# Scatters of expert rows issued in pairs over each attention slot and over six shared blocks, in place of one burst each

## The reference

```python
x = x + cross_attention(layernorm(x), ctx_1024, ctx_1024, mask, heads=16)      # 8 x 512 x 1024 scores a head
# feed-forward on xf = layernorm(x), 4096 tokens:
ys = geglu(xf @ Ws1 + bs1) @ Ws2 + bs2                                         # the shared expert, hidden size 512
top_val, top_idx = top_k((xf @ Wr + br) / 1.5, 2);  top_w = softmax(top_val)   # 2 of 12 experts for each token
yE = geglu(xf @ We1[e] + be1[e]) @ We2[e] + be2[e]                             # an expert e, hidden size 768
x = x + ys + sum over the two chosen experts of top_w * yE
```

## Time and profile before

| what | before |
|---|---|
| runs | 1084.34 to 1089.44 us, median 1086.86 |
| profiled execution, span | 1085.2 us |
| PE busy | 957.5 us (88%) |
| DVE, ACT, POOL busy | 714.1, 569.3, 373.7 us |
| DMA | 117.34 MB, mean 108 GB/s |

### The profile page before, as it was taken

One profiled execution on the slowest core, in us unless ns is written; L12 is line 12 of the kernel. 1 busy time (PEld: TensorE's weight loads), 2 busy tenths in 40 slices (PEclk: granted clock), 3 DMA queues, 4 the chain that ended last, 5 costly groups with the idle time before them and its releaser, 6 DMA issues.

```text
span 1085.2 us, 26548 instructions
## 1 busy us (share of the span) xinstructions
PE 957.5 (88%) x7515; PEld 696.9 (64%) x7515; DVE 714.1 (66%) x1842; ACT 569.3 (52%) x1276; POOL 373.7 (34%) x537
## 2 busy tenths in 40 slices
PE   5588899989888887979399889999989999999996
PEld 4233445535354344758188778888768888898885
DVE  5776778878676735646078557776636677667753
ACT  3136565655545565323054457667535667657653
POOL 5300212344443453132700044445323345335342
PEclk9779999999999999989589989999999999999999
DMA  4552315263362142144463473545324355435332
GB/s 152 132 105 81 95 55 137 90 149 86 104 157 62 41 144 74 60 148 150 153 221 117 140 216 52 140 123 144 48 33 128 49 139 138 94 85 138 48 54 42
DMA packets 107927, 117.34 MB, mean 108 GB/s; under 512 B 20396, under 2 KB 99960, under 8 KB 107648
## 3 DMA queue, kind: packets, MB, share of 16 engines
q1 hardware_dynamic: 87168, 67.97, 23.4%
q0 software_dynamic: 20064, 47.20, 17.6%
q10 hardware_dynamic: 560, 0.53, 0.1%
HBM read 73.91 MB, written 38.87 MB: 104 GB/s over the span
## 4 chain that ended last, share of the span: by engine, by line
PE 40%; issue 5%; DMA 3%; DVE 3%; another core or an unknown queue 2%; ACT 1%; DVEq 1%; SPq 0%; ACTq 0%; POOL 0%; POOLq 0%
PE ff_psH L2300 24%; PE ff_psY L2327 13%; PE ff_psX L2254 2%; DVE ff_actf L2553 1%; PE ff_psH L2269 1%; DMA out_dram<-ff_x 1%; DMA ff_xrow<-expert_in 1%; DMA expert_in<-ff_zeros 1%; PE ff_psY L2284 1%; DVE ff_actl L2546 1%; DMA ff_x<-out_dram 1%; ACT ff_gel L2394 0%; DVE ff_ysb L2629 0%; DVE ff_x L2570 0%
## 5 line engine op out<-in xcount | busy, mean ns | idle before, releaser
L2300 PE MATMUL ff_psH<-xh,ff_wx 128*128 128x256 f16 (+1 forms) x1776 | 271.0, 264 | 15.1 <-issue 9.7
L1126 DVE TENSOR_REDUCE fast_negm<-fast_psS 128x2 f32<-128x512 f32 x256 | 168.5, 686 | 85.0 <-PE fast_psS L514 75.4
L2300 PE MATMUL ff_psH<-xl,ff_wx 128*128 128x256 f16 (+1 forms) x888 | 218.7, 264 | 0.0
L886 ACT ACTIVATE fast_PT<-fast_psT 128x512 f32<-128x512 f32 x256 | 147.3, 596 | 119.9 <-PE fast_psT L546 102.2
L2235 POOL DMA_INDIRECT out_dram<-ff_ysc,ff_trow x78 | 125.6, 1610 | 194.0 <-ACT ff_ysc L2442 175.4
L2300 PEld LDWEIGHTS ff_psH<-xh,ff_wx 128*128 128x128 f16 x1776 | 167.5, 99 | 37.2 <-issue 13.9
L2553 DVE SCALAR_TENSOR_TENSOR ff_actf<-ff_psH,ff_b1T,ff_gel 128x256 f32<-128x256 f32 (+1 forms) x234 | 106.0, 454 | 101.4 <-ACT ff_gel L2394 99.7
L2394 ACT ACTIVATE ff_gel<-ff_psH,ff_b1T 128x256 f32<-128x256 f32 (+1 forms) x234 | 105.4, 451 | 82.5 <-PE ff_psH L2300 62.8
L514 PE MATMUL fast_psS<-fast_Kz,fast_Qs 128*128 128x512 f16 x256 | 101.8, 403 | 35.1 <-DVE fast_negm L1126 25.0
L2327 PE MATMUL ff_psY<-ff_wx,ff_acth 128*128 128x256 f16 x792 | 132.2, 273 | 0.6 <-DVE ff_actl L2546 0.5
L2389 ACT ACTIVATE ff_acth<-ff_actf 128x256 f16<-128x256 f32 (+1 forms) x282 | 110.5, 392 | 33.3 <-DVE ff_actf L2553 31.3
(11 more groups left out here) (276 smaller groups left out, 1672.6 us busy)
## 6 DMA issues: line engine op xcount, KB each, us to landing
ff_st<-in_L_ffn_We_dram POOLq DMA_DIRECT2D x12, 1536.0 KB
ff_xrow<-expert_in SPq DMA_DIRECT2D x41, 256.0 KB
ff_st<-in_L_ffn_We_dram POOLq DMA_DIRECT2D x12, 768.0 KB
fast_Qs<-qstk SPq DMA_DIRECT2D x48, 128.0 KB
fast_xbuf<-in_x_dram SPq DMA_DIRECT2D x8, 512.0 KB, 5.1
fast_words<-in_mask_BxSxS_bk_dram SPq DMA_DIRECT2D x8, 512.0 KB, 3.7
fast_xres<-in_x_dram SPq DMA_DIRECT2D x8, 512.0 KB, 4.1
out_dram<-fast_x1s SPq DMA_DIRECT2D x8, 512.0 KB, 5.1
```

Source lines behind the costliest of these rows:

```text
L886: nc.scalar.activation(PT[:, n % NPT, :], psT[n % 2][:], ACT.Exp).then_inc(sem["exp_done"], 1)
L1126: nc.vector.tensor_reduce(negm[:, two(b), t, 2 * p:2 * p + 2], src, AX.X, ALU.max, negate=True).then_inc(sem["max_done"], 1)
L2300: mm = nc.tensor.matmul(psH[j % stage.banks][:, (half + 1) * NB - rows:(half + 1) * NB], a[:, dt, lo:lo + P], x[:, dt, NB - rows:], start= ...
```

## The change

In each slot of POOL, `rows_out` and `meta` move to the front, behind `rstd2_`, and the eight scatters go out in four pairs: behind `meta`, behind `keep_x1`, and two behind `res_bias` that wait for the 11th and the 17th exponential of batch b. In `feed_forward()` each of the 12 pairs waits for a gate of its own: two pairs a block in blocks 2 to 7 (`act` in place of `y_mm`). The value that `place_value` reads is masked to 17 bits, which doesn't change it.

```diff
@@ -1477,10 +1477,10 @@
                 ins = nc.gpsimd.tensor_tensor(x1s[:, t, :], xres[:, t, :], keep["bs2"][:], ALU.add)
             ins.then_inc(sem["acc_done"], 1)
 
-        def scatter(b):
+        def scatter(b, these=range(2 * QT)):
             until(pool, "place_link", of("place_link", b, 5), alone=True)
-            for t in range(QT):
-                for k in range(2):
+            for n in these:
+                    t, k = n // 2, n % 2
                     pool.indirect_dma_start(out=scratch["xs"][:, :],
                                             out_offset=bass.IndirectOffsetOnAxis(ap=pos[two(b)][:, k, t:t + 1], axis=0),
                                             in_=xn2_of(b)[:, t, :], in_offset=None, bounds_check=X_ROWS - 1)\
@@ -1564,21 +1564,32 @@
             return
 
         def slot(b):
+            moved = real(b - 3) and not left_over(b - 3)
+
+            def rows_of_two(j, after=None):
+                if moved:
+                    if after:
+                        until(pool, "exp_done", of("exp_done", b, after))
+                    scatter(b - 3, (2 * j, 2 * j + 1))
+
             if real(b - 2):
                 rstd2_(b - 2)
+            if real(b - 4) and not left_over(b - 4):
+                rows_out(b - 4)
+            if moved:
+                meta(b - 3)
+            rows_of_two(0)
             if real(b):
                 sum_words(b)
             if real(b + 3):
                 rstd1(b + 3)
             if real(b - 2):
                 keep_x1(b - 2)
+            rows_of_two(1)
             if real(b - 1):
                 res_bias(b - 1)
-            if real(b - 4) and not left_over(b - 4):
-                rows_out(b - 4)
-            if real(b - 3) and not left_over(b - 3):
-                meta(b - 3)
-                scatter(b - 3)
+            rows_of_two(2, 11)
+            rows_of_two(3, 17)
 
         constants()
         rstd1(0)
@@ -1824,7 +1835,7 @@
 PIECES = 2 * EX_PAIRS
 PIECE = WCOLS // PIECES
 NSH = N // NB - EARLY
-LEFT_FROM = 3
+LEFT_FROM = 2
 FIRST_PIECES = 4
 LAST_PIECES = FIRST_PIECES + PIECES // SH_PAIRS
 
@@ -1971,8 +1982,9 @@
         return rowmeta[:, bass.ds((n & 1) * NBT, NBT), :]
 
     def place_value(eng, e):
-        return nc.values_load(place_i[0:1, bass.ds(e, 1)], engines=[eng.engine], min_val=0, max_val=(NBLK * PLACE + PLACE) * OVER - 1,
+        value = nc.values_load(place_i[0:1, bass.ds(e, 1)], engines=[eng.engine], min_val=0, max_val=(NBLK * PLACE + PLACE) * OVER - 1,
                                skip_runtime_bounds_check_because="built on chip from counts whose sum is two rows a token")
+        return value & (PLACE * PLACE * OVER - 1)
 
     def place_of(eng, e, value=None):
         value = place_value(eng, e) if value is None else value
@@ -2197,8 +2209,8 @@
         nc.gpsimd.tensor_copy(last[:, :, D + 1], mix[2][:])
         nc.gpsimd.tensor_tensor(last[:, :, D + 2], mix[1][:], mix[2][:], ALU.subtract).then_inc(meta_link, 1)
         pool.wait_ge(meta_link, 6)
-        shared.until(pool, "y_mm", of(shared, "y_mm", LEFT_FROM))
         for t in range(LEFT * QT):
+            shared.until(pool, "act", of(shared, "act", LEFT_FROM + t // 2, t % 2 * (SH_PAIRS // 2)))
             for k in range(2):
                 pool.indirect_dma_start(out=xs[:, :], in_=keep["xn2"][:, NT - LEFT * QT + t, :], in_offset=None,
                                         out_offset=bass.IndirectOffsetOnAxis(ap=last_pos[:, k, t:t + 1], axis=0),
```

## The result

In the set of runs that the prediction is held against, the changed kernel took 1055.74 us, median of 4 runs (1054.67 to 1057.44), and the kernel before 1085.96, median of 4 (1084.34 to 1089.44). The ratio is 0.972, with a 95% interval of 0.9691 to 0.9748: 2.8% faster. The forecast was 1048 with a range of 1037 to 1073. Later sets on other chips, further down, show that this gain exists on some chips only; that is the main thing that the experiments found.

A forecast was written before the change was run, and what follows sets the result against it. Back-to-back scatter bursts were taken as the bound, making other engines late. From the profiled 1085.2 us, minus 26.4 (hole) and 17.7 (slots), plus 4.8 (pairs) and 0.6 (mask), gave 1046.5; plus 1.7 for the runs, 1048 us, range 1037 to 1073.

The forecast's parts named there:

- The present bound: Attention slots and shared stage: while many scatters are queued back to back, other engines get instructions or semaphores late.
- The hole: Shared stage: the block beside the burst of 24 scatters takes 35.10 us instead of 8.7; spreading them gains 26.4 us.
- The slots: Attention slots 3 to 7: 17.7 us gained without bursts, 12.7 in slots 3 to 5 and 5 in slots 6 and 7.
- Twelve pairs in the shared stage: Shared blocks: each of 12 scatter pairs costs 0.15 us in its new place, part of 4.8 us for all 32 pairs.
- scatters in twos: Sign that the forecast holds: after the change the scatters go out two at a time.
- The moved load of expert 1's weights: Shared stage: the load moves to the middle of block 7, about 543 us, 47 us before its use; cost 0.
- POOL's order in the slots: Attention slots: `meta` and pairs ahead of POOL's other work are covered by its existing waits; cost 0.
- the mask: Place value: one more register instruction per expert on PE, ACT and DVE, 0.05 us times 12, 0.6 us lost.
- Pairs keep a short burst's share: Rival, slots and shared stage: each of 32 pairs loses 0.97 us, 31 us in all, giving 1074 us; chance 0.14.
- The hole belongs to the place: Rival, shared stage: fetching code at PE's and DVE's loop entry causes the hole, so only slots gain; 1072 us, chance 0.06.
- Nothing changes: Rival: the loss goes with each scatter and is paid again wherever scatters stand; 1087 us, chance 0.07.
- Slower: Rival, 5 slots and 6 blocks: every pair stops the engines, 2.0 us each, 63 lost against 44.1 gained; 1106 us, chance 0.05.

The follow-up runs named there:

- e5: The kernel before with the mask on the place value as its only edit, on chip 13; 1048.96 us against 1048.95 for the kernel before, ratio 1.0009.
- e1: Changed kernel, but the shared stage scatters its 24 in one burst as before (pairs in the slots only), on chip 5; 1050.49 us, ratio 1.0018 to the kernel before.
- e6: The changed kernel, unchanged, run once more on chip 13; 1049.02 us, ratio 1.0004 to the kernel before.
- e4: Changed kernel with the load of expert 1's weights issued ahead of the shared stage's first pair, on chip 5; 1049.85 us, ratio 1.002 to the kernel before.
- e8: Changed kernel with the shared stage's 24 scatters in groups of four, eight and twelve, on chip 4; 1062.48 us beside 1084.04 for the kernel before, ratio 0.9789.

## Why the prediction was right, and where it was not

*The present bound.* Right for the profile that it was read from: the bursts stopped the other engines, and what they waited for was no data. I left open whether instructions or semaphores came late. For DVE's 21.5 us it was not the data, which had moved 19 us earlier; between its signal and its instructions the traces still can't choose. For PE a signal is not enough: twelve matmuls without a wait between them took 12.6 us in place of 1.2. It was wrong to take the stall for a property of the kernel. It belongs to the kernel on certain chips, and no view of one profile could have shown that.

*The hole, -26.4.* Measured -26.6.

*The slots, -17.7, less 20 pairs at 0.15, net -14.7.* Measured -15.1, with slot 3 to 5 at 44.4, 45.0 and 42.5 and the clock at 1.00. The sum hides two misses that cancel: slots 3 to 5 gained 12.5 us where 12.7 less 12 pairs, 10.9, was forecast, and slots 6 and 7 gained 2.6 where 5 less 8 pairs, 3.8, was. Slots 6 and 7 differ by more than that between kernels on calm chips (76.5 us in e5, 83.1 in e1), so that this agreement is partly luck.

*Twelve pairs in the shared stage, +1.8.* Too small. The windows from 3 to 9 take 54.9 us in the changed kernel's stalling profile and 51.7 in e6, the same program on chip 13: 3.2 us. The step that failed is "scatters in twos": from block 3 on they went in fours. That true pairs would have cost less there is argued, since no run had them.

*The moved load of expert 1's weights, 0.* This term failed, and it makes most of the miss: 7.0 us in one window, 5.4 with the next one, which is 1.6 shorter. I had asked only whether the weights come in time (they do; ACT converts them from 584 on) and not what 2.3 MB in flight do to others. SP's store of 256 KB took 10.5 us to land beside them. On chip 13 the same kernel has 13.03 and 10.10 us in these two windows where e4, with its load far ahead, has 8.87 and 11.87: 2.4 net. And e5, with the load one block earlier, loses 2.5 (11.34 against 8.87). So 2.5 us are the load's on a calm chip, with or without the change, and the stalling set has 5.4. In the kernel before no shared block after the hole shows any of it (8.35 to 8.88 us): it lay under the hole, a cover that the change took away.

*POOL's order in the slots, 0, and the mask, +0.6.* Slots of slot 2's length bear out the first; e5's ratio of 1.0009 (0.9982 to 1.0036) can't tell 0.6 us from nothing.

*The sum.* 1048 against 1055.7; of the profiled spans, 1046.5 against 1054.4, 7.9 us. The load makes 5.4 of them, the shared pairs 1.4 (3.2 for 1.8), the experts 1.8 (2.4 for 0.6), and the hole and the slots give back 0.6; the rest is rounding. For the experts' 2.4 no cause is shown; the stretch behind window 10 to 11, which they fill, takes 471.6 to 476.0 us in the other kernels, whose work there is the same.

*The rivals.* "Pairs keep a short burst's share" (1074) is out by the slots. "The hole belongs to the place" (1072) is out as it stood, by the 8.47 us window and by e8's 8.30; but a place acts together with the number in a way that I can't name. "Nothing changes" (1087) was right in its ratio on two sets that could test it, 1.0004 on chip 13 and, by halves, 1.0018 and 1.0003 on chip 5, and for a reason that the prediction didn't have: there is nothing to remove. "Slower" had a chance of 0.05; the changed kernel is slower in neither of its two sets (0.972, and 1.0004 with 0.9981 to 1.0028).

*What was to show it.* Right: slot lengths and clock, DVE's 21.5 us wait gone, and PE without an issue wait from 490 to 545 us. Wrong: "no shared block over 11 us" (15.88), and the wait for an unnamed releaser is gone only as the one long wait, with 8.5 us left in four; "scatters in twos" and "expert stage as long as before" (2.4 us longer) failed too.

## What to carry to other kernels

An idle time that ends on nothing the profile can name is a reason to look at a second chip before explaining it: here the same program took 1047 or 1084 us, and a change worth 2.8% on one was worth 0.0% on the other. When a step that hides a stall is taken away, list the transfers that ran under it, and ask of each whom it will hold up in the open: a load of 2.3 MB was early enough for its reader and still cost 5.4 us, and sent in six parts it cost next to nothing. A wait without a name is not yet a stall: see whether the same wait has a name in a run whose landings are on record. Spacing is worth what its gates make of it: look at how far apart they really lie against how long POOL needs for what stands behind each.

## What the runs showed of the hardware that was not expected

- On some chips, or in some sets, engines go on late while GpSimd's scatters are queued: DVE 19 us after the data of its load had moved, ACT 7.4 us behind PE, and PE itself with 12.6 us for twelve matmuls that wait for nothing between them. On the calm chips 5 and 13 the same 24 scatters in a row in the same place, at the same 1.28 us pitch, left PE busy for all of its 8.30 and 8.29 us.
- Where it happens it is not proportional to the scatters: 24 cost 26.6 us, eight 9, four 0.5, twelve at another place 0.9, and three pairs that stood alone 0.2 together.
- In the stalling sets landings are missing from the record where scatters are queued: 74 against 652 beside the 24 scatters, and none missing ahead of the first scatter (2101 against 2100).
- One load of 2.3 MB made a store of 256 KB land after 10.5 us in the stalling set and 8.1 to 8.3 on calm chips (e5, e6), where the list of issues has 3.3 us as the median in e5 from 494 to 526, with 24 scatters beside it.
